# A two-layer attention and expert kernel: GpSimd's work cut into pieces, the inverse roots spread over four slots, and TensorE's units for the next pair of heads put ahead of the weighted sums

## What is computed

```
x = x + attention0(norm(x)) + experts0(norm(x))    16 heads of 64, unit-length q and k, 2 null keys, distance bias, causal
x = x + attention1(norm(x)) + experts1(norm(x))    16 heads of 8, rotary q and k, causal
experts: route each token to its top 2, up to a capacity; y = sum of weight * expert(token)
```

## Time and profile before

| | |
|---|---|
| median of 3 runs | 1981.93 us (1979.71 to 1986.19) |
| profiled execution | 1989.61 us, of it the span from first to last instruction 1987.8 us |
| mean granted PE clock over the span | 0.908 of 2.4 GHz |
| first attention | about 217 to 1259 us |
| second attention (`attend1`) | about 1532 to 1988 us |

### The profile page before, as it was taken

The page is one execution under the profiler, slowest core; times in us unless marked ns, Lnnn a source line. Parts: engine busy times, 40 slices in busy tenths (PEclk is TensorE's granted clock), DMA queues, the critical chain, the costliest instruction groups (busy, mean ns, idle before and its releaser), DMA issues. The chain is left out here.

```text
span 1987.8 us, 36054 instructions
## 1 busy us (share of the span) xinstructions
PE 1592.0 (80%) x13931; PEld 804.5 (40%) x13931; DVE 1155.7 (58%) x2098; ACT 885.3 (45%) x1438; POOL 832.8 (42%) x476
## 2 busy tenths in 40 slices
PE   1468549879999898899988998345997888898888
PEld 1235424435455454544535443223654323323332
DVE  6313347785565655556575560481166889768971
ACT  0112214535656464565645455022321666546666
POOL 1500463564676757668676879260001111400000
PEclk9779858989999999999999999567998999869999
DMA  4113210000000000000000000123321001000000
GB/s 160 51 35 94 59 25 14 11 6 23 12 13 18 13 23 7 25 7 18 18 13 16 10 18 6 67 79 98 96 68 34 11 14 31 9 12 8 2 10 14
DMA packets 57110, 62.01 MB, mean 31 GB/s; under 512 B 12890, under 2 KB 42862, under 8 KB 56046
## 3 DMA queue, kind: packets, MB, share of 16 engines
q1 hardware_dynamic: 52846, 51.32, 8.2%
q0 software_dynamic: 4096, 8.40, 1.6%
HBM read 40.34 MB, written 18.48 MB: 30 GB/s over the span
## 5 line engine op out<-in xcount | busy, mean ns | idle before, releaser
L1584 POOL TENSOR_TENSOR a_prob_sum<-a_prob_sum,a_prob 128x1024 f32<-128x1024 f32 (+2 forms) x224 | 486.0, 2170 | 164.5 <-ACT a_prob L1532 143.6
L1532 ACT ACTIVATE a_prob<-a_st,a_table 128x512 f32<-128x512 f32 (+3 forms) x640 | 351.8, 626 | 309.7 <-PE a_st L1410 155.3
L1652 DVE TENSOR_REDUCE a_maxima<-a_ring 128x16 f32<-128x512 f32 (+3 forms) x640 | 353.5, 600 | 172.6 <-PE a_ring L1342 128.4
L1935 DVE TENSOR_REDUCE a_maxima<-a_mx 128x1 f32<-128x512 f32 (+3 forms) x640 | 353.1, 604 | 80.9 <-PE a_mx L1927 39.5
L1437 PE MATMUL a_ot<-a_prob,a_values 128*64 128x512 f32 (+3 forms) x1280 | 279.1, 553 | 0.0
L2191 ACT ACTIVATE a_prob<-a_st 128x1024 f32<-128x1024 f32 x224 | 216.6, 1022 | 96.6 <-PE a_st L2106 77.2
L1919 PE MATMUL a_mx<-a_ks,a_qs 32*128 32x512 f16 (+3 forms) x640 | 174.9, 369 | 44.7 <-DVE a_maxima L1935 39.2
L1342 PE MATMUL a_ring<-a_k_hi,a_q_hi 64*128 64x512 f16 (+3 forms) x640 | 156.1, 369 | 61.7 <-DVE a_maxima L1652 38.8
L1410 PE MATMUL a_st<-a_q_hi,a_k_hi 64*128 64x512 f16 (+4 forms) x704 | 129.9, 336 | 0.0
L2122 PE MATMUL a_ot<-a_prob,values_all 128*32 128x512 f32 x896 | 128.9, 649 | 0.2 <-ACT a_sums L2182 0.2
L1410 PE MATMUL a_st<-a_q_lo,a_k_hi 64*128 64x512 f16 (+4 forms) x704 | 128.8, 334 | 0.0
(11 more groups left out here) (265 smaller groups left out, 2683.0 us busy)
## 6 DMA issues: line engine op xcount, KB each, us to landing
a_rden<-rden_wide SPq DMA_DIRECT2D x64, 128.0 KB, 2.9
f_w<-in_w SPq DMA_DIRECT2D x28, 256.0 KB, 2.9
expert_in<-zeros SPq DMA_DIRECT2D x5, 1024.0 KB, 11.1
f_rows<-expert_in SPq DMA_DIRECT2D x16, 256.0 KB, 3.4
expert_out<-f_result SPq DMA_DIRECT2D x16, 256.0 KB, 2.2
shared_w<-in_w SPq DMA_DIRECT2D x12, 256.0 KB, 2.9
a_table<-in_head_table SPq DMA_DIRECT2D x16, 140.5 KB, 2.2
parts<-part_t SPq DMA_DIRECT2D x4, 512.0 KB
```

The lines of the kernel that those rows point to most:

```text
L1532: e = act.activation(prob[:, s % NPROB, a, c0:QW], ps_st[s % 2][:, a, c0:QW], ACT.Exp, bias=table[x][:, a, at:at + 1])
L1584: pool.tensor_tensor(into[:, :, c0:QW], into[:, :, c0:QW], here[:, :, c0:QW], ALU.add).then_inc(added, 2 if r == TPQ - 2 else 1)
L1652: dve.reduce_max(maxima[:, qt // TPQ, a, qt % TPQ, at:at + count], bank[:, 0:hi - lo].rearrange("p (w k) -> p w k", k=WINDOW), AX_X).then_ ...
L1935: dve.reduce_max(own.maxima[:, qt // TPQ, a, qt % TPQ, n:n + 1], bank[:, 0:hi - lo], AX_X).then_inc(done, 1)
```

## The change

It has four parts. In the first attention the list `two` is issued ahead of both weighted sums of its pair of slots instead of behind them, and the parts 0 to 3 of the inverse roots stand in slots 23, 24, 25 and 26, one in each; POOL's wait stays in slot 25. In the second attention POOL clears only the columns of `prob_diag` that ACT doesn't write, in 12 operations, and PE waits for them ahead of its second weighted sum, ACT no longer; and the multiplication and addition of the fetched rows are 64 operations of 128 columns instead of 3.

```diff
--- before.py
+++ after.py
@@ -919,7 +919,7 @@
 FIRST0 = Ahead0(0)
 AFTER_FIRST0 = Ahead0(19)
 NEXT0 = Ahead0(9)
-NEXT0.newton = {ENDS0[2]: (0,), ENDS0[2] + 1: (1, 2, 3)}
+NEXT0.newton = {ENDS0[2] + k: (k,) for k in range(NEWTON + 1)}
 POOL_NORM0 = {ENDS0[3]: (0, 1), ENDS0[0]: (2, 3)}
 FIRST_V_AT0 = {QK_UNITS0 + u: u for u in range(V_UNITS0)}
 FIRST_TRANS_AT0 = {15 + g: g for g in range(NQB)}
@@ -1455,6 +1455,9 @@
                             scores(x, m % NS0)
                     if n % 2 == 1:
                         for m in (n - 3, n - 2):
+                            if m == n - 3:
+                                for unit in two:
+                                    put(unit, base, 2 * i + unit.what[0], i)
                             if (m < 0 and first) or m >= 2 * NS0:
                                 continue
                             px, ps = divmod(m, NS0)
@@ -1462,8 +1465,6 @@
                             if SLOTS0[ps][1] == 0 and not (first and m == 0):
                                 pe.wait_ge(ot_read, i * (2 * NQB) + NQB * px + SLOTS0[ps][0])
                             weighted(px % 2, ps)
-                    for unit in two:
-                        put(unit, base, 2 * i + unit.what[0], i)
 
             pe.wait_ge(zeroed, ZEROED0)
             pe.wait_ge(halves_loaded, 16 * HALF_LOADS0)
@@ -2065,18 +2066,20 @@
 
         @block.gpsimd
         def _(pool):
-            pool.memset(prob_diag[:, :, :, :], 0.0).then_inc(left_zero, 1)
+            for r in range(1, TPQ):
+                for a in range(HPG1):
+                    pool.memset(prob_diag[:, r - 1, a, 0:P * r], 0.0).then_inc(left_zero, 1)
             for c in range(CHOICES):
                 pool.wait_ge(exp_done, 2 * (GATHER_FROM1 + GATHER_EVERY1 * c))
                 pool.indirect_dma_start(back[:, c, :], None, mem.expert_out[1][:, :],
                                         bass.IndirectOffsetOnAxis(ap=mem.slot_from[1][:, c:c + 1], axis=0)).then_inc(gathered, 16)
             pool.wait_ge(gathered, 16 * CHOICES)
-            weights = mem.weights[1][:, :].unsqueeze(2).to_broadcast([P, CHOICES, D])
-            pool.tensor_tensor(back[:, :, :], back[:, :, :], weights, ALU.mult).then_inc(combined, 1)
-            for k in range(2):
-                pool.wait_ge(combined, k + 1)
-                pool.tensor_tensor(mem.acc[:, :, :], mem.acc[:, :, :], back[:, NT * k:NT * k + NT, :],
-                                   ALU.add).then_inc(combined, 1)
+            for c in range(CHOICES):
+                weights = mem.weights[1][:, c:c + 1].to_broadcast([P, D])
+                pool.tensor_tensor(back[:, c, :], back[:, c, :], weights, ALU.mult).then_inc(combined, 1)
+            for c in range(CHOICES):
+                pool.wait_ge(combined, CHOICES + (c - NT + 1 if c >= NT else 0))
+                pool.tensor_tensor(mem.acc[:, c % NT, :], mem.acc[:, c % NT, :], back[:, c, :], ALU.add).then_inc(combined, 1)
 
         @block.tensor
         def _(pe):
@@ -2118,6 +2121,8 @@
                 pe.wait_ge(exp_done, 2 * m + 2)
                 if kt == 0 and m > 0:
                     pe.wait_ge(ot_read, nth_block(g, qb))
+                if m == 1:
+                    pe.wait_ge(left_zero, (TPQ - 1) * HPG1)
                 for a in range(HPG1):
                     mm = pe.matmul(ps_ot[32 * a:32 * a + 32, :], values_all[:, g, kt, a, :], prob_of(m)[:, a, :],
                                    start=kt == 0, stop=kt == TPQ * qb + TPQ - 1)
@@ -2181,7 +2186,6 @@
                 act.wait_ge(pv_done, n)
                 act.activation(sums[:, qb % 2, :], ps_ot[:, :], ACT.Copy).then_inc(ot_read, 1)
 
-            act.wait_ge(left_zero, 1)
             for n in range(ALL1):
                 (qb, kt), c0 = SLOTS1[n % NS1], first_col(n % NS1)
                 for half in range(2):
@@ -2237,7 +2241,7 @@
                 elif kind == "proj":
                     acc = mem.acc[:, TPQ * qb:TPQ * qb + TPQ, :].rearrange("p t d -> p (t d)")
                     if qb == 0:
-                        dve.wait_ge(combined, 3)
+                        dve.wait_ge(combined, 2 * CHOICES)
                     dve.tensor_tensor(acc, acc, bank[:, :], ALU.add).then_inc(ring_done, 1)
 
             for qb in range(TURNS_BEFORE1):
```

## The result

| | before | after |
|---|---|---|
| median | 1981.49 us (1979.71 to 1991.47, 6 runs) | 1998.88 us (1994.53 to 2006.08, 6 runs) |
| profiled execution | 1989.61 us | 2006.08 us |
| granted PE clock | 0.908 | 0.914 |

The ratio is 1.0083, with a 95% interval of 1.0055 to 1.0112: 0.8% slower, where 0.4% faster was forecast, and outside the range of 1957 to 1989 us.

A forecast was written before the change was run, and what follows sets the result against it. PE was taken to bound the first attention, a ring of PE, DVE and ACT the second. First attention 56 - 43 = 13 us longer, less 4.6 and 17: 8 us off the median 1981.9 gives 1974 us, range 1957 to 1989.

The forecast's parts named there:

- Turning ahead of the sums: First attention, pairs 1 to 6: the sums fill PE's wait between turning products, 24 x 1.1 = 26 us gained.
- Roots over four slots: First attention, slots 24 and 25: den's wait shrinks and PE's clock holds, 3.3 us in each of five pairs, 17 us gained.
- out in slot 18: First attention: the projection waits for POOL's product with the sums behind it; 13 us lost, plus 7 for the clock.
- out in slot 30: First attention: the projection waits for POOL, delayed 2.4 us by roots part 3; 16 us lost, plus 7 for the clock.
- out in slot 10: First attention: the projection waits for POOL's product; 3.5 us lost in five pairs, 6 us in pairs 6 and 7.
- Clearing in pieces: Start of the second attention: DVE's small L2205 no longer ends with POOL's whole clearing; 4.6 us gained.
- Combining in pieces: Second attention, group 1, slots 28 to 39: DVE waits for one piece at most and PE's clock holds; 17 us gained.
- the new waits cost more than I charge: Rival, 12%: in slot 25 POOL's late start holds ACT, then PE, in pairs 1 to 5; 1989 us.
- fall to half clock in the second attention: Rival, 12%: a short wait still brings PE down there, saving only 3.0 of the 17 us; 1988 or 1992 us.
- get in between the pieces: Rival, 4%, second attention: DVE doesn't, so L2205 waits for POOL's whole series, from 1725 to 1751; 2011 us.

The follow-up runs named there:

- after_roots_early: The changed kernel with the four parts of the roots in slots 21 to 24 instead of 23 to 26; 1997.31 us, ratio 1.0075.
- order_only: The kernel before with the first attention's new order alone, roots and second attention as before; 2010.34 us, ratio 1.0132.
- out_behind: The changed kernel with the projections put back behind the weighted sums; 1947.79 us against 1981.35 of the kernel before, ratio 0.9808.
- turn_ahead: As out_behind, with the q/k products also back behind the sums, only turnings and v ahead; 1941.76 us, ratio 0.9791 to the kernel before.
- combine_only: The kernel before with only the second attention's combining in pieces, the clearing whole; 1977.13 us against 1979.73, ratio 0.9979.
- roots_only: The kernel before with only the roots spread over slots 23 to 26; 1975.17 us against 1981.35, ratio 0.9954.
- roots3_only: The kernel before with only the roots' parts in slots 23, 24 and 25 (one, one and two); 1965.85 us against 1982.27, ratio 0.9931.

## Why the prediction was wrong

The mechanisms of the prediction were nearly all there; four sizes and one omission turned -8 us into +17. By its own steps, with the sums over pairs 1 to 7:

- **Turning ahead of the sums**: predicted -26, measured -18. A place gives back about 0.75 us, not 1.1: at most the 0.81 of idle time could go, and part of it returns as waits for maxima (0.29 us ahead of `v` and 0.36 ahead of `out` in slot 6, in each pair). The 1.1 counted the whole distance to the ideal start.
- **Roots over four slots**: predicted -17, measured -12 (-11 alone). den's wait is 0.84 us as said. Its fall in clock is cheaper or rarer than the five-times-1.8 charged from one pair: slots 24 and 25 of that pair ran at 0.85 still.
- **out in slot 18**: predicted +20, measured +14.5. PE waits 1.84 us in pairs 1 to 5, where 2.3 were forecast, and 3.76 in pairs 6 and 7. The place costs 1.3 us in pairs 1 to 3, not 1.9, and 3.0 in pairs 4 and 5, where the clock fell behind it: two of five, where five were charged.
- **out in slot 30**: predicted +24 with the clock, measured +34. The wait was right (3.3 predicted, 2.8 to 3.5 measured), and so was its cause, POOL late through part 3: after_roots_early takes 16 us of it away. Two things were mis-sized. The fall of the clock costs 2.6 us (out and sums, 5.7 against 3.1), not 1.4. And pairs 6 and 7, charged 0.8, lose 5.8, in order_only 7.4 already, with no roots made. Pair 7 had a wait of 2.46 us for POOL's product there before and has 4.32 now. Besides, the prediction put nearly all of slot 30 down to POOL's lateness; order_only, with POOL on time, loses 16 of the 34 us there by the order itself.
- **out in slot 10**: predicted +9.5, measured +11.0. In pairs 1 to 5, 3.6 of it go with the q/k products ahead, as out_behind shows.
- **q/k ahead**: not charged; measured +5.4 in slots 14 to 17. turn_ahead shows that it is the q/k products ahead that wait.
- **Clearing in pieces**: predicted -4.6; PE's idle time there went from 10.00 to 5.28 us, -4.7, as forecast. **Combining in pieces**: predicted -17, measured -6 by the stretches and -3 (-8 to -1) by combine_only.

This last is the largest single failure: 11 us. The difference between two stretches of one execution was taken off the median, and the text did so knowing that this execution was 7.7 us above it. The clock's long fall, some 11 us more than in roots_only or order_only, makes up that surplus. Had it been weighed so, the sum would have been +3, that is 1985 us: no gain, but within the range. The other errors of size (+8 turning, +5 roots, +10 slot 30, +5 q/k, +1 slot 10, -5 slot 18) make the rest, and more. The measured terms, with pair 0 (+3) and the end behind slot 38 of pair 7 (-2), add up to 34 + 3 - 2 - 5 - 6 = 24 us and the medians differ by 17; the profiled execution of after was itself 7.2 us above its median. That remainder was not taken apart.

Of the rivals, "the new waits cost more than I charge" was right in direction, but its mechanism, ACT held by POOL's additions, was not what showed: POOL's product itself held PE, and in slot 30 also the order and the clock. PE did not fall to half clock in the second attention, and DVE did get in between the pieces.

## What to carry to other kernels

A unit that waits for another engine's late result belongs behind work that does not wait. Moving a group of units ahead as one mixes those that gain (the turnings, 18 us) with those that lose (the projections, some 50); ask of each kind alone what it waits for. When a stretch of the profiled execution is charged for its clock, compare that execution with the median first: a surplus of the same size is a sign that the stretch is not typical. And a helper's work placed in a gap of another engine's (the roots in the two slots without an addition) may be safe only there; look at what runs beside it before it is spread.

## What the hardware showed unexpectedly

- The same wait of 2.9 to 3.0 us of PE in the second attention was followed by a clock of 0.54 over 48 us in one execution and of 0.86 over 36 to 37 us in three others (roots_only, order_only, roots3_only). In the changed kernel a wait of 1.84 us in slot 18 was followed by a fall of the clock in two of five pairs, and in order_only a wait of 0.8 us in slot 30 in three of the same five.
- DVE's small operations on SBUF were held by a running addition of POOL: a TENSOR_SCALAR of 128x64 took 2.31 us and a TENSOR_TENSOR of 128x64 took 1.78 us, each 0.2 us alone. Reductions from PSUM were not: six of 128x512 took 3.68 us beside additions in the changed kernel, two of them 1.29 us without. The Trainium skill (SBUF — State Buffer, Who interferes with whom) says that `tensor_scalar` can enter the modes that contend for the ports shared with GpSimd, that an instruction with two SBUF inputs contends with one of GpSimd that reads SBUF, and that `tensor_reduce` never contends. The traces agree: the first two kinds were held, the third was not.
- GpSimd's pieces of 128 columns cost 461 ns for an addition and 395 ns for a multiplication, where 0.47 us was estimated for an addition; the 64 of them were hidden: slots 28 to 39 of group 1 took 30.62 us at clock 1.00 beside them.
